# A decoder block in fp32 on one core: recurrent stage in PSUM, scales by head on ScalarE, bias rows in two rounded parts, another order of work

## What is computed

```python
x = x + xattn(layernorm(x), ctx)     # self-attention, cross-attention over 2048 keys, relu MLP
x = x + rwkv_block(layernorm(x))     # below
x = x + expert_attn(layernorm(x))    # 8 heads of 64, top 2 of 5 value and output experts

# rwkv_block: time axis is the batch axis, so only two steps, t = 0 and 1
xr, xw, xk, xv, xa, xg = (x + (xprev - x) * m for m in mus)
r, k, v = xr @ Wr, xk @ Wk, xv @ Wv
w = exp(-exp(-softplus(-(w0 + xw @ Ww)) - 0.5));  a = sigmoid(a0 + xa @ Wa);  g = sigmoid(xg @ Wg)
kk = normalised by head(k * k_k);  k = k * (1 + (a - 1) * k_a)
S = S * w + S @ ab(kk, a) + outer(v, k);  y = S r
y = norm_by_head(y) * lnx_w + lnx_b + sum_by_head(r * k * r_k) * v
h = layernorm(x + (y * g) @ Wo);  out = layernorm(silu(h @ Wf + bf))
```

## Time and profile before

| what | us |
|---|---|
| median of 3 runs | 256.61 (254.85 to 259.63) |
| the profiled execution, its time | 256.62 |
| its span, first to last instruction | 254.9 |
| TensorE busy (share) | 232.1 (91%) |
| VectorE busy | 165.0 (65%) |
| ScalarE busy | 86.7 (34%) |
| GpSimd busy | 87.3 (34%) |

### The profile page before, as it was taken

How to read it: one execution, slowest core, us unless ns; L and a number is a source line. 1 busy time by engine, 2 the same in 40 slices (tenths; PEclk the granted TensorE clock), 3 DMA queues, 4 the chain that set the end, 5 groups by cost and what they waited for, 6 DMA issues and landing times.

```text
span 254.9 us, 3033 instructions
## 1 busy us (share of the span) xinstructions
PE 232.1 (91%) x1153; PEld 161.0 (63%) x1153; DVE 165.0 (65%) x309; ACT 86.7 (34%) x144; POOL 87.3 (34%) x81
## 2 busy tenths in 40 slices
PE   3899989999999999999899999995886789799995
PEld 3888758789888786885644433331442359599861
DVE  2234571785659786813827747779954759999962
ACT  2061123346197768121062264312101021432210
POOL 5020042220839623720402054866511213345000
PEclk9999999999999999999999999998999799999999
DMA  7999599253984199399000599000000000000002
GB/s 249 433 400 419 229 454 401 85 199 141 431 356 167 37 377 397 136 411 431 24 0 0 221 427 383 1 1 0 0 0 0 3 0 0 0 3 1 3 0 82
DMA packets 6350, 43.98 MB, mean 173 GB/s; under 512 B 832, under 2 KB 832, under 8 KB 1472
## 3 DMA queue, kind: packets, MB, share of 16 engines
q1 hardware_dynamic: 6336, 43.80, 42.6%
HBM read 43.27 MB, written 0.52 MB: 172 GB/s over the span
## 4 chain that ended last, share of the span: by engine, by line
PE 68%; DVE 17%; POOL 8%; issue 3%; ACT 3%; POOLq 0%; DVEq 0%
PE psum L386 63%; PE psum L390 4%; POOL slots L1661 4%; ACT slots L1407 3%; DVE slots L1099 2%; DVE slots L826 2%; POOL small L1652 1%; DVE slots L1102 1%; DVE slots L816 1%; DVE small L808 1%; DVE small L1112 1%; PE psum L502 1%; DVE ring L1151 1%; POOL small L1736 1%; DVE ring L1107 1%
## 5 line engine op out<-in xcount | busy, mean ns | idle before, releaser
L386 PE MATMUL psum<-ring,slots 128*128 128x512 f32 (+3 forms) x228 | 94.5, 562 | 6.6 <-ACT slots L1407 3.5
L386 PEld LDWEIGHTS psum<-ring,slots 128*128 128x128 f32 (+1 forms) x228 | 40.6, 196 | 51.1 <-issue 38.6
L1407 ACT ACTIVATE slots<-psum 128x512 f32<-128x512 f32 (+3 forms) x51 | 27.5, 551 | 109.4 <-PE psum L386 59.2
L386 PE MATMUL psum<-slots,ring 128*128 128x128 f32 x448 | 52.7, 277 | 2.3 <-ACT slots L1407 2.3
L386 PEld LDWEIGHTS psum<-slots,ring 128*128 128x128 f32 x448 | 51.1, 192 | 3.8 <-ACT slots L1407 3.3
L386 PE MATMUL psum<-ring_r,slots_r 128*128 128x512 f32 x192 | 46.2, 396 | 0.0
L1657 POOL TENSOR_TENSOR ring_r<-ring,ring_r 128x640 fp32r<-128x640 f32 x16 | 31.8, 2005 | 38.9 <-ACT ring_r L1407 38.9
L386 PEld LDWEIGHTS psum<-ring_r,slots_r 128*128 128x128 f32 x192 | 35.5, 188 | 9.1 <-ACT slots_r L1407 1.0
L1652 POOL TENSOR_TENSOR small<-small,mhalf 128x1 f32<-128x1 f32 x16 | 13.6, 852 | 77.1 <-DVE small L812 77.1
L1407 ACT ACTIVATE ring_r<-ring 128x2048 fp32r<-128x2048 f32 (+1 forms) x17 | 31.5, 1865 | 13.1 <-PE psum L386 8.2
L832 DVE TENSOR_TENSOR ring_r<-ring,ring_r 128x1408 fp32r<-128x1408 f32 x16 | 26.4, 1656 | 4.3 <-ACT ring_r L1407 4.3
(11 more groups left out here) (158 smaller groups left out, 204.2 us busy)
## 6 DMA issues: line engine op xcount, KB each, us to landing
ring<-blocks SPq DMA_DIRECT2D x36, 1024.0 KB, 9.1
bc<-vecs SPq DMA_DIRECT2D x1, 3072.0 KB, 11.7
bc<-vecs SPq DMA_DIRECT2D x1, 1280.0 KB, 6.9
slots<-xin SPq DMA_DIRECT2D x2, 256.0 KB, 4.0
bc<-vecs SPq DMA_DIRECT2D x1, 512.0 KB, 14.2
y<-slots SPq DMA_DIRECT2D x2, 256.0 KB, 2.0
colv<-cols SPq DMA_DIRECT2D x1, 14.0 KB, 12.3
```

The costliest lines, as they stand in the source:

```text
L386: return t.matmul(o_, l, r, start=first, stop=last)
L1407: return a.activation(o, x, func, **kw)
```

## The change

1. **Start.** GpSimd makes the matrix of ones earlier, the causal mask and `pick` later. The order of loads is another: ct00 in front of k1 and of x of row 1, c03 and c01 in front of ct12, rg last.
2. **Counts.** VectorE adds the four counts; TensorE makes one product in place of four. `count2(0)` stands directly in front of `shut_out(0)`.
3. **Bias rows.** ScalarE rounds 64 rows of a bias (all equal) to f32r, VectorE puts the remainder into 32 of them, and one f32r product with a 64-row matrix of 1/32 adds both. Two of the five stand in front of the transposes of n4 of row 1, and both of bf behind the gate products.
4. **Recurrent layer.** VectorE and ScalarE read k, v, r and the tanh of a and g in PSUM; some results (`key_c[1]`, `y_p`) are written there, some in place. c3, c1 and the addition of lnx_b (`bonus`) go from GpSimd to VectorE. Three kinds of scaling by head (`bonus_rows` for both rows, `scales0`, `own_part`) become eight ScalarE instructions of 64 columns each (`by_head`). The waits for evictions of r and v go.
5. **Order.** On every engine instructions stand in another order: in GpSimd's queue `mixg` comes before the covariance and `sel` before the power of s; on VectorE the affine of h of row 1 comes before `silu(0)` and `done_s(1)` before `ranks(0)`; on ScalarE `select` comes before the copy of h of row 1; TensorE's scores, transposes and last products are permuted.

The diff, cut:

```diff
+        th_p, g_p = [bank(1), bank(6)], [bank(1), bank(6)]
+        key_c = [TMP[0], bank(6)]
+        k_p, r_p, v_p = [bank(2), kt[1]], [bank(0), bank(4)], [bank(3), bank(5)]
+        y_p = [bank(2), bank(7)]
+        W0, A0, BF, FREE = BCAST.index("w0"), BCAST.index("a0"), 0, BCAST.index("fc2_b")
+        row_parts = {"a0": (W0, 0), "w0": (A0, 64), "bf": (FREE, 0)}
...
             eng.dma_start(X[0], xin[0, :, :]).then_inc(s_x[0], 16)
             fetch("q1")
+            fetch("ct00")
+            fetch("k1")
             eng.dma_start(X[1], xin[1, :, :]).then_inc(s_x[1], 16)
-            fetch("k1")
-            fetch("ct00")
             fetch("v1")
             fetch("ct01")
+            fetch("ct02")
+            fetch("q2")
+            fetch("k2")
             eng.dma_start(bc[:, 0:2, :], spread(0, 2)).then_inc(s_bc0, 16)
-            fetch("k2")
-            fetch("q2")
+            eng.dma_start(bc[:, 2:FIRST_BC, :], spread(2, FIRST_BC)).then_inc(s_bc1, 16)
+            fetch("ct11")
             fetch("ct03")
-            fetch("ct02")
             fetch("ct10")
-            eng.dma_start(bc[:, 2:FIRST_BC, :], spread(2, FIRST_BC)).then_inc(s_bc1, 16)
+            fetch("c03")
+            fetch("c01")
             fetch("ct12")
-            fetch("ct11")
-            eng.dma_start(colv[:, :], cols).then_inc(s_cols, 16)
...
-            fetch("c01")
-            fetch("c02")
             fetch("ct13")
...
             fetch("fg")
-            fetch("fo")
-            s.wait_ge(*used("c11"))
-            fetch("rf")
+            fetch("rg")
...
             def bias(name, bk):
-                mm(bank(bk), ones[0:1, :], vec(name)[0:1, :], True, False)
+                i, p = row_parts[name]
+                s.wait_ge(*rows_a.at("share"))
+                s.wait_ge(*rows_v.at(name))
+                mm(bank(bk), share[p:p + 64, :], bc_r[p:p + 64, i, :], True, False)
...
-                for n in range(4):
-                    s.wait_ge(*counted[b].at(str(n)))
-                    i = mm(psum[:, bk, 0:1], ones[0:1, :], cnt4[b][0:1, n:n + 1], n == 0, n == 3)
-                i.then_inc(*prod[b].inc("n2"))
+                s.wait_ge(*counted[b].at("sum"))
+                mm(psum[:, bk, 0:1], ones[0:1, :], cnt[b][0:1, :], True, True).then_inc(*prod[b].inc("n2"))
...
-            q2(1)
+            k2(1)
             count2(0)
-            k2(1)
             shut_out(0)
...
+            s.wait_ge(*p_low[1].at("3"))
+            s.wait_ge(*evict[1].at("relu"))
+            bias("a0", 6)
             step(0, "k", 1, 2)
+            s.wait_ge(*y_in[1].at("3"))
+            bias("w0", 7)
             turned_rows(1, "n4", N4[1], 4)
             step(0, "v", 2, 3, wait=y_in[0].at("3"))
             step(1, "k", 0, 5, wait=evict[1].at("relu"))
-            s.wait_ge(*p_low[1].at("3"))
-            s.wait_ge(*evict[1].at("relu"))
-            bias("a0", 6)
             step(1, "a", 1, 6, bias_of="a0")
             step(0, "r", 3, 0, wait=turned[0].at("n4"))
...
             step(1, "r", 3, 4, wait=turned[1].at("n4"))
-            s.wait_ge(s_bc2, 16)
-            s.wait_ge(*evict[0].at("r"))
-            bias("bf", 0)
             step(1, "v", 4, 5, wait=evict[1].at("k"))
-            s.wait_ge(*evict[1].at("r"))
+            step(0, "g", 4, 1, wait=rk_v[0].at("c"))
+            step(1, "g", 5, 6, wait=rk_v[1].at("km"))
+            s.wait_ge(*rk_v[1].at("ys"))
+            s.wait_ge(*rk_v[1].at("c3"))
+            s.wait_ge(*rk_v[1].at("c1"))
             s.wait_ge(s_bc2, 16)
             bias("bf", 4)
-            step(0, "g", 4, 1, wait=evict[0].at("th"))
-            step(1, "g", 5, 6, wait=evict[1].at("th"))
             s.wait_ge(*rk_v[0].at("yg"))
...
+            def sum_counts(b):
+                for m in four:
+                    s.wait_ge(*counted[b].at(m))
+                v.tensor_reduce(cnt[b][0:1, :], cnt4[b][0:1, :], AX.X, ALU.add).then_inc(*counted[b].inc("sum"))
...
+            def row_low(name):
+                i, p = row_parts[name]
+                low_rows = slice(p + 32, p + 64)
+                s.wait_ge(*rows_a.at(name))
+                v.tensor_tensor(bc_r[low_rows, i, :], vec(name)[low_rows, :], bc_r[low_rows, i, :],
+                                ALU.subtract).then_inc(*rows_v.inc(name))
...
+            def bonus(b):
+                s.wait_ge(*by_a[b].at("pv"))
+                v.tensor_tensor(pv[b], v_p[b], vec("lnx_b"), ALU.add).then_inc(*rk_v[b].inc("pv"))
...
+            bonus(0)
             read_keys(1)
-            sum_read(1)
-            s.wait_ge(*own_v.now())
-            v.reciprocal(keep["rn"], keep["rn"]).then_inc(*rk_v[1].inc("rn"))
-            s.wait_ge(*rk_g[1].at("c3"))
+            s.wait_ge(*prod[1].at("r"))
+            s.wait_ge(*rk_g[1].at("a"))
+            v.tensor_tensor(th[1], r_p[1], th[1], ALU.mult).then_inc(*rk_v[1].inc("c3"))
+            s.wait_ge(*prod[1].at("r"))
+            s.wait_ge(*rk_g[1].at("w"))
+            v.tensor_tensor(w1, r_p[1], w1, ALU.mult).then_inc(*rk_v[1].inc("c1"))
...
+            s.wait_ge(*by_a[1].at("sc"))
+            v.tensor_tensor(y_p[1], y_p[1], ys[1], ALU.add).then_inc(*own_v.inc())
+            s.wait_ge(*own_v.now())
+            v.tensor_tensor(y_p[1], y_p[1], vec("lnx_w"), ALU.mult).then_inc(*own_v.inc())
+            bonus(1)
             s.wait_ge(*own_v.now())
             s.wait_ge(*rk_g[1].at("rs"))
-            v.tensor_tensor(heads(ys[1]), heads(sc_[1]), over(rs8[1], 64), ALU.mult).then_inc(*own_v.inc())
-            add_bonus(1)
+            v.tensor_tensor(heads(y_p[1]), heads(y_p[1]), over(rs8[1], 64), ALU.mult).then_inc(*own_v.inc())
+            s.wait_ge(*rk_v[1].at("pv"))
+            s.wait_ge(*own_v.now())
+            v.tensor_tensor(ys[1], y_p[1], pv[1], ALU.add).then_inc(*own_v.inc())
             gated(1)
...
             out_o(1)
             norm_h(1)
+            affine(1, "h", hn[1], TMP[1], "norm_b")
             silu(0)
-            affine(1, "h", hn[1], TMP[1], "norm_b")
...
             logits(0)
+            done_s(1)
             ranks(0)
-            done_s(1)
...
+            def share_out():
+                s.wait_ge(*const.at("ones"))
+                for b in range(2):
+                    s.wait_ge(*energy_in[b].at("nb1"))
+                act(share[:, :], ones[:, :], ACT.Copy, scale=1.0 / 32).then_inc(*rows_a.inc("share"))
+            def row_high(name, loaded_):
+                i, p = row_parts[name]
+                s.wait_ge(*loaded_)
+                act(bc_r[p:p + 64, i, :], vec(name)[p:p + 64, :], ACT.Copy).then_inc(*rows_a.inc(name))
...
+            def by_head(b, name, o_, x, factor):
+                for h in range(8):
+                    cs = slice(h * 64, (h + 1) * 64)
+                    i = act(o_[:, cs], x[:, cs], ACT.Copy, scale=factor[:, h:h + 1])
+                i.then_inc(*by_a[b].inc(name))
...
             s.wait_ge(*const.at("wbias"))
             s.wait_ge(*prod[1].at("w"))
             act(w1, bank(7), ACT.Tanh, scale=0.5).then_inc(*evict[1].inc("w"))
...
-            act(TMP[1], vc[1], ACT.Square).then_inc(*sq_a[1].inc("vc"))
-            mix1("g", 5)
-            tanh(0, "g", "g", gt[0], 1)
+            act(TMP[1], vc[1], ACT.Square, scale=0.125).then_inc(*sq_a[1].inc("vc"))
+            own_part()
+            tanh(0, "g", "g", g_p[0], 1)
+            bonus_rows(1)
+            tanh(1, "g", "g", g_p[1], 6)
             copy_turned(0, "yg", T16, 1, scale=0.5)
-            tanh(1, "g", "g", gt[1], 6)
             copy_turned(1, "yg", T16, 5, scale=0.5)
             copy_turned(0, "h", T10, 3)
             silu(0)
+            select()
             copy_turned(1, "h", T10, 7)
...
-            mul(pv[0], pv[0], vec("lnx_b"), rk_g[0], "pv", ALU.add)
-            s.wait_ge(*rk_g[1].at("a"))
-            s.wait_ge(*evict[1].at("r"))
-            mul(th[1], th[1], rt[1], rk_g[1], "c3")
-            s.wait_ge(*rk_g[1].at("w"))
-            s.wait_ge(*evict[1].at("r"))
-            mul(w1, w1, rt[1], rk_g[1], "c1")
             s.wait_ge(*rk_v[1].at("ys"))
             s.wait_ge(*rk_v[1].at("rn"))
             mul(sc_[1], ys[1], vec("r_k"), rk_g[1], "sb")
+            s.wait_ge(*own_g.now())
+            mul(rs8[0], rs8[0], ss[0], rk_g[0], "rs")
+            s.wait_ge(*mixed[1].at("g"))
+            mixg = MIX[1][1].rearrange("p (c n) -> p c n", c=4)
+            mul(mixg, mixg, bcols(T8, 1), mixed_g, "g", ALU.add)
...
-            g.tensor_tensor(heads(pv[1]), heads(vt[1]), over(sbs[1], 64), ALU.mult).then_inc(*own_g.inc())
-            s.wait_ge(*own_g.now())
-            s.wait_ge(*rk_v[0].at("sb"))
-            mul(heads(sc_[0]), heads(vec("lnx_w")), over(rs8[0], 64), rk_g[0], "sc")
-            s.wait_ge(*mixed[1].at("g"))
-            mixg = MIX[1][1].rearrange("p (c n) -> p c n", c=4)
-            mul(mixg, mixg, bcols(T8, 1), mixed_g, "g", ALU.add)
...
-            deviation(0, "s")
-            deviation(0, "n5")
-            deviation(1, "s")
```

(24 more changed lines are left out.)

507 lines of the change are left out of this document (257 added, 250 removed).

## The result

| | before | changed |
|---|---|---|
| median of the runs | 258.12 us (254.85 to 262.1, 4 runs) | 247.46 us (245.78 to 251.22, 4 runs) |
| the profiled execution: its time, its span | 256.62, 254.9 us | 247.14, 245.4 us |
| VectorE, ScalarE, GpSimd busy | 165.0, 86.7, 87.3 us | 162.7, 92.8, 75.5 us |

The ratio of the times is 0.965, with a 95% interval from 0.958 to 0.972: the changed kernel is 3 to 4% faster. Forecast were 245.3 us and a range of 241.5 to 251.5. Executions of one kernel differ in how much of them TensorE spends at its lower clock; the ratio is taken over the least disturbed ones.

What follows compares the result with a forecast made beforehand. TensorE, busy 91% of the 254.9 us span, was taken as the bound; gains at the front, in bias products and from closed gaps brought the span to 243.6, plus 1.7 around it: 245.3 us, range 241.5 to 251.5.

Steps and rivals of the forecast that it cites:

- Start and first layer: Front, to 47 us: ones made earlier and ct01 moved; first work at 2.3, scores at 44.0, 2.2 us gained.
- Cross-attention: Counts, scores and gathers to 110 us: cheaper counts, the rest only permuted; the 2.2 us lead becomes 2.75.
- Bias rows: Bias products on TensorE: 0.25 us each against 1.05; 0.5 us before row 1's n4 transposes, 4.2 us behind them.
- rival B: Closed gaps return as VectorE waits if PSUM writes and part of the reads cost double: 250 to 251 us; chance 0.18.
- D: Slower: instructions in place in PSUM cost three times the usual on row 1's gate chain, 262 us; chance 0.04.
- ScalarE series: Recurrent stage: scaling by head as four series of eight 64-column slices, 1.75 us a series, 3.1 at the dear end.
- The gap of 2.88: Wait before the last gate product: closes with mixg earlier and 8.7 us off GpSimd, and 1.5 us of lower clock goes.
- Gated rows: Row 0's gated result at 171.2 and row 1's at 177.0; TensorE waits 0.4, then 0.9 us for VectorE.
- After the gates: After the recurrent stage: waits of 2.08 and 1.60 go; nearly 3 us idle before rf(1), then priced at 5.2.
- A: Likeliest case, whole kernel as summed: 245.3 us, own range 242 to 248; chance 0.62.
- E: Late gains fail because another GpSimd wait replaces mixg; front and biases remain, 250 us; chance 0.04.
- C: Late loads: transfers 2 us late at three places give 251 us, more makes it 252 to 254; chance 0.12.

Runs made afterwards that it cites:

- Again: The changed kernel run a second time with no edit, its profiled execution at full clock throughout (span 243.7 us): 247.17 us, ratio 0.967.
- two such edits: On the kernel before: mixg ahead of the covariance, 260.65 us; the affine of h row 1 ahead of silu(0) with done_s(1) ahead of ranks(0), 260.78 us.
- the third: The kernel before with one order edit alone, GpSimd making ones first: 260.51 us, ratio 1.018.

## Why the prediction came out as it did

The mechanism and the sign were right; by the marks the 245.3 is the sum of two errors that partly cancel. At n4 of row 1 the changed kernel is 4.2 us behind the forecast, and from there to the last addition (242.21 against 251.72 before) it gains 11.5 us where 9.1 were summed. Of these 2.4 us more, 1.0 stand between h and n5 of row 0: the stretch at the lower clock that was priced after rf(1) didn't come. In the run with the earlier count it came, and that piece took 13.3 us instead of 12.4, where 13.4 were summed. So a part of the closeness is luck.

**Start and first layer: right.** First work 2.46 (2.3), scores 43.72 (44.0). The affine of the line with 2.11 us took 0.75 once GpSimd's subtraction stood elsewhere, and the gap of 0.86 is gone.

**Cross-attention: a gain of 2.75 was written, none came.** Three terms failed. The wait before `shut_out(0)` was 0.99, not 0.6. The steps "only permuted" were costed at nothing: on VectorE the last split of weights now stood behind a subtraction that overlaps GpSimd's, and 0.59 and 1.15 us of waiting came in; the earlier trace rows show such an overlap for another pair. Third, the clock: it costs the first trace 1.5 us after the short wait. "Again", without it, is still 2.05 behind the forecast at 109.65, though its scores began 0.44 early: 1.73 by the splits, 0.28 by `shut_out`, and 0.5 that I could not place.

**Bias rows: right kind, wrong size.** 0.43 on TensorE, not 0.25; the two before n4 of row 1 make the 0.36 us that the mark lacks beyond that. The nearest row, f32r products at 0.23, has many in sequence; this is a single one between fp32 products, with its weight load; which of these makes the difference no run shows. Undoing the form costs 2.2 us, where four at 0.8, 3.2 us, were priced. From n4 of row 1 to yg of row 0 "again" takes 31.9 us where it was 41.0: 3.8 by bias products, 2.9 by the wait, 1.5 by the clock, and 0.9 without a name.

**PSUM: right.** Four results in place in PSUM and one from another bank (`key_c`) took 0.69 to 0.70 us, so rival B's and D's price doesn't exist. The run with `y_p` in SBUF shows the same from the other side. The Trainium skill (VectorE: DVE Perf Modes, The TRN2 errata) would have put 0.06 us on each instruction with a PSUM source; by this trace (0.69 beside 0.69 from SBUF) it doesn't show.

**ScalarE series: right.** 1.71, 1.98, 1.98 and 1.68 us against 1.75. The two written in place in PSUM are the short ones, but those written in SBUF took 2.02, so the place of the result does not make the 0.3 us. The source in SBUF remains as the likely cause; no run has a series that reads PSUM and is not in place. The prediction's estimate of 1.9 from the Trainium skill (ScalarE: Activation LUTs, What ACT_TABLE_LOAD costs) lies between them.

**The gap of 2.88: right in size, its cause left unsplit.** The prediction named the place of `mixg` and the 8.7 us taken off GpSimd together. The two runs from both sides show that this edit is worth 1.1 us on the changed kernel and 0.4 on the kernel before, where VectorE's gate was next. The other 1.8 us need the rest of the change. Of the 8.7 us taken off GpSimd only 2.7 stand between the covariance and `mixg`; the covariance itself waited for VectorE, and comes 4.3 us earlier. Before, three bias products stood between n4 of row 1 and the v of that row, none do now, and v is read in PSUM with no copy to wait for; no run parts these. What kept the wait from coming back at the gated rows was, by 2.2 us, the series on ScalarE.

**Gated rows: better than summed.** The forecast had waits of 0.4 and 0.9; there is none. In "again" VectorE's gated rows end at 172.23 and 177.56, 0.55 and 0.1 us before they are asked for. It is a near thing: four products more give 1.93 us of waiting.

**After the gates.** The wait of 2.65 before rf(1) came as forecast ("nearly 3"). The clock after it did not (3.70, not 5.2 us), and the run with `sel` early shows that the wait hides a chain of the same length, so it cost nothing by itself. One reading of the code was wrong: GpSimd's expert products stand behind its power in both kernels. What left the place of the earlier trace rows's 3.06 us norm was `sel`: with the late order on the kernel before, where `sel` keeps its place, the norm still took 3.06 us. In the changed kernel it took 1.28 us, and n5 of row 1 is turned without a wait, as forecast.

**Rivals.** A held, with the time 2.2 us above it. B, D and E are excluded by the prices and marks above. Of C, no product of TensorE waited for a load by the trace; ScalarE waited for two (0.75 us before the split at 60.07, 3.69 us before row bf at 148.74), and neither held TensorE up. The margin of 0.2 us at k1 was as thin as forecast: in the runs with the series on VectorE and with the old bias products TensorE waited 0.31 and 0.19 us for that block at 11.5 us.

## What to carry to other kernels

Closing a wait by order pays only if the engine that is late next has slack: on the kernel before, two such edits moved their waits by one step, the third passed its 1.8 us on, and none made the time shorter; with work taken off GpSimd and VectorE and the bias products out of the way, the waits before the last gate product and the gated rows went for good. Give an instruction on the second-latest engine a price even where the list of steps is "only permuted", above all where VectorE's and GpSimd's subtractions come to overlap. And judge a change of 1% by the marks of a trace with the clock at full, not by times that hold one or two stretches at the lower one.
